# Half rows of the adjacency: read from a bf16 copy in DRAM, or cast from f32 by the load

## The chip, the cores and the metric

One core of a Trainium2 chip runs the whole program; the other cores do nothing. The metric is the device time of one execution in microseconds. The kernel before took 1334.71 us, the median of three runs (1331.9 to 1335.75).

## What is computed

Four graph layers over 2708 nodes with 256 features and one dense 0/1 adjacency, each as x = x + layer(relu(layernorm(x))). Layer 1 is the one that the change touches. The node and edge adjacencies are the same matrix, its diagonal cleared first:

```python
node_adj_norm = node_adj.at[idx, idx].add(-dn)
edge_output = _gru_cell(node_adj_norm @ h, h, edge_Wih, edge_Whh, ...)
# one of three heads
e_plus = leaky_relu(concatenate([hp, hm], axis=1) @ a, ALPHA)[:, 0]
att = jnp.where(edge_adj > 0, e_plus[None, :], NEG_INF)
att = softmax(att, axis=1) * edge_adj @ hW
```

The softmax needs, for each row and head, the maximum of e_plus over the row's neighbours. That is a product of an adjacency row with a row of scores, and a maximum over it.

## The kernel before

The nodes are padded to 2816 = 22 blocks of 128 (NT = 22). A transposed adjacency stays on chip as fp8 (AT), and most of the work reads it. Row maxima need the other orientation, with a node's neighbours along the free dimension; that is what the half rows are for.

The work runs in stages. **Layer 0** is attention with four heads. It has 8 units (two groups of 11 blocks, four heads) of 22 steps. In a step ACT makes thresholds (L811), DVE turns them into masks with the adjacency (L1130, L1136), and PE multiplies 11 blocks by 4 small matmuls of 65 columns (L1619). DVE evicts a unit in the middle of the next (from L1147) and, in the later units, also widens AT (L1171). SP loads a broadcast row of scores for each unit (load_el, L422). POOL meanwhile loads the second half of AT with a cast (L686). Then, paced by the masks built, it casts the 22 row blocks of the f32 adjacency to bf16 and writes them back to DRAM, into AH_D (L689). SP waits for all of these (L465), clears the diagonal of AH_D with one scattered DMA of two-byte elements (L466), and waits for that.

The **edge GRU** has 22 steps. In each, PE multiplies the node sums (L1665), the head products (L1677, L1679) and the gates (L1710, L1717), and DVE and ACT split and evict. POOL computes delta(t) (L703), which needs ACT's tanh (L876) of the same step, and apply(t-1) (L708, L709), in this order. Between these DVE computes the paired maxima, those of heads 0 and 1: 88 maxima over half rows of 1408 elements (row_max, L1316). rows_before(t) spreads them over 20 steps, 4 or 5 in each. In step t DVE runs the step's first maximum, the blend of step t-1 (L1349, L1350), more maxima, support_low and products_low (L1289, L1295, L1298), the step's last maximum, and gru_new (L1340, L1342).

Maximum i of the paired ones uses half row L = i // 2. The half rows lie in two buffers, AROW[:, L % 2], and load L may start once maxima_after(L - 2) = 2(L - 1) maxima are done. SP issues them (load_row, L483 to L488) in its own order among the loads and stores of the step, each behind its wait for that count.

The **attention** has 9 units (three heads, three groups of blocks) of 22 steps m. PE multiplies (L1760, L1761), while ACT and DVE make the weights. The 44 maxima of head 2 are run by DVE at the steps in row_at, one every 9/4 steps, and SP issues the loads there too. What follows is a node GRU, layer 2 and a test of whether layer 3 is needed at all.

Of the kernel before, what the change touches and what calls it, by code (L numbers as in the profile page):

```python
# [8 lines left out]
BF16 = mybir.dt.bfloat16  # L9
# [9 lines left out]
def gnn_stack_kernel(nc, t_in, out):  # L19
# [60 lines left out]
    with ExitStack() as ctx:  # L80
        def sb(name, shape, dt=F32):
            return ctx.enter_context(nc.sbuf_tensor(name, shape, dt))
# [3 lines left out]
        def sem(name):  # L86
            if name not in sems:
                sems[name] = ctx.enter_context(nc.semaphore(name))
            return sems[name]
# [68 lines left out]
        RD = a0.take(11)  # L158
        ZB = a0.take(NT, dt=BF16, size=2)
        NOTB = a0.take(P, dt=FP8, size=1)  # L160
# [7 lines left out]
        HTF = AT[:, :, htf_at:htf_at + 4 * H0 * C0].bitcast(F32)  # L168
        assert NREAL <= (P - 1) * NT
        THRi = THR.bitcast(mybir.dt.int32)  # L170
# [94 lines left out]
        DN = sb("DN", [P, NT])  # L265
        NOTI = sb("NOTI", [P, P])
        identh = sb("identh", [P, P], F16)
# [15 lines left out]
        MN_D = nc.dram_tensor("m_rows", [H1, NT, P], F32, kind="Internal").ap()  # L283
        AH_D = nc.dram_tensor("adj_rows_half", [NT, P, N], BF16, kind="Internal").ap()
        HT_D = nc.dram_tensor("h_turned", [P, NT, 4 * P], F16, kind="Internal").ap()
# [67 lines left out]
        def rows_before(t):  # L353

            return min(PAIRED, -(-PAIRED * t // ROWS_LAST))

        def loads_before(t):

            return max(2, -(-rows_before(t) // 2))

# [7 lines left out]
        def half_of(L):  # L368

            i = L % (2 * NT)  # L370
            return i // 2, i % 2

        def maxima_after(L):

            return 2 * (L + 1) if L < 2 * NT else PAIRED + L + 1 - 2 * NT

        def diagonal_half(t):

            return t // (NT // 2)
# [32 lines left out]
        def _(sp):  # L412
# [49 lines left out]
            def load_halves(to, k, name):  # L462
                sp.dma_start(to, WS_D[k]).then_inc(sem(name), 16)

            sp.wait_ge(sem("rows_h"), 16 * NT)  # L465
            sp.dma_start(AH_D.rearrange("t p n -> (t p n)")[0:(P - 1) * NT * (N + 1)]  # L466
                         .rearrange("(a b c) -> a b c", b=NT, c=N + 1)[:, :, 0:1],
                         ZB[0:P - 1, :].unsqueeze(2), allow_slow_non_contiguous=True).then_inc(sem("rows_z"), 16)
            sp.wait_ge(sem("rows_z"), 16)
            for i in range(4):  # L470
# [11 lines left out]

            def load_row(L):  # L483
                t, c = half_of(L)
                if L >= 2:
                    sp.wait_ge(sem("rmax"), maxima_after(L - 2))
                sp.dma_start(AROW[:, L % 2, :], AH_D[t, :, c * QUARTER:(c + 1) * QUARTER]
                             ).then_inc(sem(f"arow{L % 2}"), 16)  # L488

            def load_scores(to, h):  # L490
# [3 lines left out]
            for t in range(NT):  # L494
                sp.wait_ge(sem("h1"), t + 1)
                sp.dma_start(H_D[:, t, :], H32R[:, t % 8, :]).then_inc(sem(saved_sem(t % 8)), 16)
                if t == 10:
                    load_halves(GWS, 0, "we")
            for L in range(2):
                load_row(L)  # L500
            sp.wait_ge(sem("hts_act"), NT // 2)
# [36 lines left out]
            for t in range(NT):  # L538
                if t + 2 < NT:
                    load_h(t + 2, HR, 0)  # L540
                for L in range(loads_before(t + 1) if t else 2, loads_before(t + 2)):
                    load_row(L)
                if t == NT - 2:
                    save_maxima(0, 2)
                    load_maxima(0)
                sp.wait_ge(sem("hw_lo"), (H1 + 1) * (t + 1))
                sp.dma_start(HW_D[:, :, t, :].rearrange("h p c -> p h c"), HWS[:, t % 2, :, :]
                             ).then_inc(sem(f"hwst{t % 2}"), 16)
                if t == NT - 2:
                    sp.wait_ge(sem("ns_lo"), DC * len(SUP))  # L550
                    sp.wait_ge(sem("nb_mm"), 1)
                    sp.wait_ge(sem("ht_saved"), 16)
                    for i in range(2):
                        sp.wait_ge(sem(f"hwst{i}"), 16 * 9)
                    for c in range(3):
                        load_products(0, c)
            for L in range(2 * NT, 2 * NT + 2):
                load_row(L)
            for i in range(2):
# [11 lines left out]
            for m in range(len(units1) * NT):  # L571
                n, j = divmod(m, NT)
                h, g = units1[n]
                if m in row_at and row_at[m] + 2 < 4 * NT:
                    load_row(row_at[m] + 2)
                if m + 6 in check_at:
# [67 lines left out]
        def _(pool):  # L644
# [9 lines left out]
            pool.memset(ALR, 0.0).then_inc(sem("consts"), 1)  # L654
            link(pool.memset(ZB, 0.0))
            pool.memset(ET[:], 1.0).then_inc(sem("consts"), 1)
# [27 lines left out]
            for t in range(NT):  # L684
                pool.wait_ge(sem("masks_built"), 3 * t + 1)
                pool.dma_start(AT[:, t, GA[0][1] * P:NT * P], adjT[t, :, GA[0][1] * P:NT * P]).then_inc(sem("adj_b"), 16)  # L686
            for t in range(NT):
                pool.wait_ge(sem("masks_built"), 68 + 4 * t)
                pool.dma_start(AH_D[t], t_in["adj"][t * P:(t + 1) * P, :]).then_inc(sem("rows_h"), 16)  # L689

            pool.wait_ge(sem("dn"), 16)
# [3 lines left out]
            for t in range(NT):  # L695
                pool.wait_ge(sem("h1"), t + 1)
                pool.tensor_copy(HHL[:, t, 0, :], H32R[:, t % 8, :]).then_inc(sem("hi1"), 1)

            def delta(t, base, hr, n):

                pool.wait_ge(sem(f"hr{t % 4}"), 16 * (saved_count(t % 4) + (t // 4 + 1) + (len(range(t % 4, NT, 4)) if base else 0)))
                pool.wait_ge(sem("n"), base + t + 1)
                pool.tensor_tensor(hr[:, t % 4, :], hr[:, t % 4, :], n[:, t % 2, :], ALU.subtract).then_inc(sem("delta"), 1)  # L703
# [6 lines left out]

            for t in range(NT + 1):
                if t < NT:
                    delta(t, 0, HR, GT)
                if t >= 1:
                    apply(t - 1, 0, HR)

            pool.wait_ge(sem("hw_mm"), NT)
            for m in range(len(units1) * NT):
                if m in piece_at:
                    i = piece_at[m]  # L720
                    which, _, c, scale = pieces2[i]
                    if i == 0:
                        pool.wait_ge(sem("rmax"), MAXIMA)
                    pool.wait_ge(sem("raw0"), 32 + [16, 32, 48, 64, 96, 128][i])
                    half = [WIH2S, WHH2S, W2S][i // 2][:, c, :, :]
                    split(RAW2, half, scale, 2 * D if which == "W2T" else 3 * D)
# [281 lines left out]
        def _(dve):  # L1008
# [294 lines left out]
            def row_max(i):  # L1303
# [10 lines left out]
                if i > 0:  # L1314
                    dve.wait_ge(sem("rmax"), i)
                dve.tensor_tensor_reduce(junk, AROW[:, L % 2, :], eb[:, c * QUARTER:(c + 1) * QUARTER], 1.0, 0.0,  # L1316
                                         ALU.mult, ALU.max, M2[:, c, h * NT + t:h * NT + t + 1]).then_inc(sem("rmax"), 1)
# [635 lines left out]
```

## Time and profile before

| | |
|---|---|
| median of 3 runs | 1334.71 us |
| the profiled execution | 1334.99 us |
| its span, first to last instruction | 1332.9 us |
| mean granted TensorE clock | 0.941 |
| busy, share of the span | PE 86%, DVE 70%, ACT 59%, POOL 16% |
| moved by the DMA engines | 153.68 MB, mean 115 GB/s |

Busy time is that of one profiled execution. "Issue" as the releaser of a wait means that the engine waited for nothing that the profile shows. PE is the matmuls and PEld the weight loads, which overlap them. In a window an instruction that crosses its edge counts in both. Times are microseconds, or nanoseconds where a mean of one is given.

### The profile page before, as it was taken

To read this page: it belongs to the slowest core of one execution; us is meant where nothing else is said; L and a number is where in the kernel's file an instruction comes from. 1 tells how busy PE (TensorE), PEld (TensorE's weight loads), DVE (VectorE), ACT (ScalarE), POOL (GpSimd) and SP (SyncE) were. 2 spreads that over 40 slices of the span, in tenths; PEclk is the share of its full clock that TensorE was granted. 3 is DMA by queue.
4 is the path that set the end of the run, shared out by engine and by line. 5 is a ranking of instruction groups with operands and counts; after the bars stand their busy time and mean duration, and the time that the engine had idled before them with its cause. 6 is when DMAs were issued, how large, how long until landed. Compare 5 with 4: busy or idle time off the path is not lost.

```text
span 1332.9 us, 35106 instructions
## 1 busy us (share of the span) xinstructions
PE 1140.3 (86%) x15054; PEld 938.5 (70%) x15054; DVE 937.4 (70%) x2037; ACT 785.0 (59%) x1001; POOL 216.7 (16%) x296
## 2 busy tenths in 40 slices
PE   5529897987886989899978999999999997778997
PEld 4429887887885767666656888888888654446886
DVE  5786677767896289999995998769995365553541
ACT  3479988777735123332226999989989465653000
POOL 5631010000003012222222000001220141220000
PEclk9759999999995789999999999999999998899999
DMA  9936565556307343434336345417852010020532
GB/s 216 180 51 67 62 95 115 98 111 128 63 4 267 94 128 100 126 104 129 104 114 210 106 147 180 135 59 286 281 193 104 5 30 16 16 95 1 180 125 86
DMA packets 83731, 153.68 MB, mean 115 GB/s; under 512 B 9537, under 2 KB 60337, under 8 KB 82609
## 3 DMA queue, kind: packets, MB, share of 16 engines
q1 hardware_dynamic: 74993, 127.05, 30.8%
q0 software_dynamic: 7392, 23.79, 12.9%
q8 instruction: 120, 1.97, 0.6%
q10 hardware_dynamic: 1184, 0.53, 0.1%
q14 instruction: 42, 0.34, 0.1%
HBM read 171.26 MB, written 35.60 MB: 155 GB/s over the span
## 4 chain that ended last, share of the span: by engine, by line
PE 56%; DVE 23%; issue 8%; ACT 6%; DMA 3%; POOL 3%; ACTq 0%; SPq 0%; DVEq 0%; POOLq 0%
PE PS L1619 18%; PE PS L1760 10%; PE PS L1761 10%; DVE scratch L1316 9%; PE PS L1814 8%; PE PS L1710 3%; POOL arena L703 2%; PE PS L1801 2%; DVE arena L1298 2%; DVE arena L1090 2%; PE PS L1717 1%; PE PS L1587 1%; DMA arena<-e_rows 1%; DVE arena L1342 1%; PE PS L1654 1%
## 5 line engine op out<-in xcount | busy, mean ns | idle before, releaser
L1760 PE MATMUL PS<-arena 128*128 128x257 f16 x1452 | 325.5, 272 | 7.6 <-ACT arena L897 4.4
L1619 PE MATMUL PS<-arena 128*128 128x65 f16 x7744 | 259.1, 196 | 80.8 <-issue 41.3
L1761 PE MATMUL PS<-arena 128*128 128x257 f16 x1452 | 325.5, 274 | 0.0
L1619 PEld LDWEIGHTS PS<-arena 128*128 128x128 fp8e4 x7744 | 256.4, 99 | 83.4 <-issue 81.6
L811 ACT ACTIVATE arena<-arena 128x1408 fp8e4<-128x1408 f32 x176 | 242.5, 1456 | 51.4 <-DVE arena L1130 51.1
L1316 DVE CUSTOM_DVE_ANT_0 scratch<-arena 128x1408 bf16<-128x1408 bf16 x132 | 223.2, 1691 | 23.7 <-DMA arena<-e_rows 11.1
L897 ACT ACTIVATE arena<-arena 128x896 int16<-128x896 uint8 (+1 forms) x198 | 187.3, 973 | 22.8 <-DVE arena L1371 14.7
L1760 PEld LDWEIGHTS PS<-arena 128*128 128x128 bf16 x1452 | 142.7, 98 | 32.6 <-issue 8.6
L1761 PEld LDWEIGHTS PS<-arena 128*128 128x128 bf16 x1452 | 139.9, 96 | 21.5
L1130 DVE TENSOR_TENSOR arena<-arena,AT 128x352 int32<-128x352 int32 x176 | 91.3, 519 | 83.4 <-PE PS L1619 63.3
L888 ACT ACTIVATE arena<-arena,E1B 128x896 uint8<-128x896 f32 (+1 forms) x131 | 139.3, 1064 | 2.0 <-DMA arena<-m_rows 2.0
L876 ACT ACTIVATE arena<-arena 128x256 f32<-128x256 f32 x44 | 18.3, 417 | 186.1 <-DVE arena L1342 186.1
L1710 PE MATMUL PS<-arena 128*128 128x512 f16 x528 | 122.3, 382 | 0.4 <-ACT PS L860 0.4
L1665 PE MATMUL PS<-AT,arena 128*128 128x256 fp8e4 x968 | 111.5, 275 | 0.0
L703 POOL TENSOR_TENSOR arena<-arena 128x256 f32<-128x256 f32 x44 | 47.4, 1076 | 377.8 <-ACT arena L876 377.8
L1814 PE MATMUL PS<-arena,AT 128*128 128x256 f16 x968 | 106.2, 273 | 0.8 <-DVE X L1466 0.8
L1665 PEld LDWEIGHTS PS<-AT,arena 128*128 128x128 f16 x968 | 95.6, 99 | 12.1
L1814 PEld LDWEIGHTS PS<-arena,AT 128*128 128x128 fp8e4 x968 | 94.6, 98 | 12.5 <-DVE X L1466 1.1
L1371 DVE TENSOR_TENSOR arena<-arena,AT 128x224 int32<-128x224 int32 (+1 forms) x198 | 80.1, 432 | 19.2 <-ACT arena L888 19.0
L1710 PEld LDWEIGHTS PS<-arena 128*128 128x128 f16 x528 | 51.8, 98 | 56.8 <-issue 2.7
L1136 DVE TENSOR_TENSOR arena<-arena,AT 128x352 int32<-128x352 int32 x176 | 90.8, 516 | 0.0
L1423 DVE SCALAR_TENSOR_TENSOR scratch<-arena 128x1408 fp8e4<-128x1408 f32 x44 | 73.2, 1664 | 0.8 <-DMA arena<-in_adj 0.8
(189 smaller groups left out, 1333.3 us busy)
## 6 DMA issues: line engine op xcount, KB each, us to landing
arena<-adj_rows_half SPq DMA_DIRECT2D x88, 352.0 KB, 3.1
arena<-in_adj SPq DMA_DIRECT2D x44, 704.0 KB, 5.3
adj_rows_half<-in_adj POOLq DMA_DIRECT2D x22, 704.0 KB, 8.3
hw_saved<-arena SPq DMA_DIRECT2D x22, 387.0 KB, 4.3
AT<-in_adjT POOLq DMA_DIRECT2D x44, 176.0 KB, 8.0
arena<-hw_saved SPq DMA_DIRECT2D x9, 774.0 KB, 5.8
arena<-el_rows SPq DMA_DIRECT2D x8, 704.0 KB, 11.5
arena<-h_saved SPq DMA_DIRECT2D x44, 128.0 KB, 2.1
```

Source lines behind the costliest of these rows:

```text
L811: act.activation(THR[:, m % NTHR, :], ELB[:, n % 2, :], ACT.Sigmoid, bias=ERB[:, j, h:h + 1], scale=SHARP, saturate=False).then_inc(sem("t ...
L888: act.activation(Y[:, m % NRING, 0:nb * P], MB[n % 2][:, 0:nb * P], ACT.Relu, bias=E1B[:, j * H1 + h:j * H1 + h + 1], saturate=False).then ...
L897: act.activation(PWb[:, m % NRING, 0:nb * P], Y[:, m % NRING, 0:nb * P], ACT.Copy, scale=256.0).then_inc(sem("p_ready"), 1)
L1130: dve.tensor_tensor(mask_words(m, 0), THRi[:, m % NTHR, :], adj_words(m), ALU.bitwise_and).then_inc(sem("m_plus"), 1)
L1136: dve.tensor_tensor(mask_words(m, 1), mask_words(m, 0), adj_words(m), ALU.bitwise_xor).then_inc(sem("masks_built"), 1)
L1316: dve.tensor_tensor_reduce(junk, AROW[:, L % 2, :], eb[:, c * QUARTER:(c + 1) * QUARTER], 1.0, 0.0, ALU.mult, ALU.max, M2[:, c, h * NT + t ...
L1619: ins = pe.matmul(PS[:, first_bank(n) + i, (2 * r + q) * C0:(2 * r + q + 1) * C0], MASK[:, (m + j) % NMASK, q, k * P:(k + 1) * P], MOV[:, ...
L1665: ins = pe.matmul(PS[:, c, 0:D], HHL[:, j, a, c * P:(c + 1) * P], AT[:, j, i0 * P:i1 * P], start=(j == 0 and a == 0), stop=(j == NT - 1 an ...
L1710: ins = pe.matmul(PS[:, bank, :], half(c, a), w[:, c, b, 0:2 * D], start=False, stop=(w is wih and c == DC - 1 and a == 1), skip_group_che ...
L1760: pe.matmul(PS[:, k, 0:D + 1], weights, w[:, 0:D + 1], start=(j == 0), stop=False)
L1761: ins = pe.matmul(PS[:, k, 0:D + 1], weights, w[:, D + 2:2 * D + 3], start=False, stop=(j == NT - 1))
L1814: ins = pe.matmul(o, AT[:, j, t * P:(t + 1) * P], YHL[:, j, a, :], start=(j == 0 and a == 0), stop=(j == NT - 1 and a == 1))
```

## The change

AH_D, its casts, its zeroing and SP's waits for them are gone. POOL issues the loads of the half rows itself, straight from the f32 adjacency; the DMA casts to bf16 on the way into AROW. Their place in POOL's program is set by three conditions around delta and apply, and in the attention by row_at. The diagonal is cleared on chip: before the first maximum that uses a half row which holds the diagonal block (head 0, and again head 2), DVE ANDs that block, 128x64 words, with NOTI, which is now bf16, and waits for the result. That makes 22 ANDs in the edge GRU and 22 in the attention.

```diff
@@ SP
-            sp.wait_ge(sem("rows_h"), 16 * NT)
-            sp.dma_start(AH_D...[:, :, 0:1], ZB[0:P - 1, :].unsqueeze(2), ...).then_inc(sem("rows_z"), 16)
-            sp.wait_ge(sem("rows_z"), 16)
...
-            def load_row(L):
-                t, c = half_of(L)
-                if L >= 2:
-                    sp.wait_ge(sem("rmax"), maxima_after(L - 2))
-                sp.dma_start(AROW[:, L % 2, :], AH_D[t, :, c * QUARTER:(c + 1) * QUARTER]
-                             ).then_inc(sem(f"arow{L % 2}"), 16)
...
-                for L in range(loads_before(t + 1) if t else 2, loads_before(t + 2)):
-                    load_row(L)
...
-                if m in row_at and row_at[m] + 2 < 4 * NT:
-                    load_row(row_at[m] + 2)
@@ POOL
-            link(pool.memset(ZB, 0.0))
...
-            for t in range(NT):
-                pool.wait_ge(sem("masks_built"), 68 + 4 * t)
-                pool.dma_start(AH_D[t], t_in["adj"][t * P:(t + 1) * P, :]).then_inc(sem("rows_h"), 16)
...
+            def load_row(L):
+
+                t, c = half_of(L)
+                if L >= 2:
+                    pool.wait_ge(sem("rmax"), maxima_after(L - 2))
+                pool.dma_start(AROW[:, L % 2, :], t_in["adj"][t * P:(t + 1) * P, c * QUARTER:(c + 1) * QUARTER]
+                               ).then_inc(sem(f"arow{L % 2}"), 16)
+
+            load_row(0)
+            load_row(1)
+            fetched = 2
...
             for t in range(NT + 1):
+                while t < NT and 2 * fetched < rows_before(t + 1):
+                    load_row(fetched)
+                    fetched += 1
                 if t < NT:
                     delta(t, 0, HR, GT)
+                while fetched < 2 * NT + 2 and maxima_after(fetched - 2) <= min(rows_before(t + 1) + 1, rows_before(t + 2)):
+                    load_row(fetched)
+                    fetched += 1
                 if t >= 1:
                     apply(t - 1, 0, HR)
+                while fetched < 2 * NT + 2 and maxima_after(fetched - 2) <= min(rows_before(t + 1) + 2, rows_before(t + 2)):
+                    load_row(fetched)
+                    fetched += 1
...
             for m in range(len(units1) * NT):
+                if m in row_at and row_at[m] + 2 < 4 * NT:
+                    load_row(row_at[m] + 2)
@@ DVE, row_max
+                if h != 1 and c == diagonal_half(t):
+                    at = t * P - c * QUARTER
+                    block = AROW[:, L % 2, at:at + P].bitcast(mybir.dt.int32)
+                    link(dve.tensor_tensor(block, block, NOTI[:].bitcast(mybir.dt.int32), ALU.bitwise_and))
                 dve.tensor_tensor_reduce(junk, AROW[:, L % 2, :], eb[:, c * QUARTER:(c + 1) * QUARTER], 1.0, 0.0,
                                          ALU.mult, ALU.max, ...).then_inc(sem("rmax"), 1)
```

## Rows read from the trace of the kernel before

**Rows 1.** The page, part 4: shares of the chain of waits by line.
```profile
PE PS L1619 18%; PE PS L1760 10%; PE PS L1761 10%; DVE scratch L1316 9%; PE PS L1814 8%; PE PS L1710 3%; POOL arena L703 2%; PE PS L1801 2%; DVE arena L1298 2%; DVE arena L1090 2%; PE PS L1717 1%; PE PS L1587 1%; DMA arena<-e_rows 1%; DVE arena L1342 1%; PE PS L1654 1%
```

**Rows 2.** Busy time by stretch: PE, PEld, DVE, ACT, POOL, clock, DMA share, GB/s.
```profile
190.00:350.00 160.00, 129.12 (x3847) 127.39 (x3844) 113.22 (x258) 123.79 (x91) 12.12 (x23) 0.97 0.62 118
...
470.00:700.00 230.00, 208.18 (x1513) 147.62 (x1512) 211.12 (x354) 66.75 (x152) 56.10 (x55) 0.98 0.39 112
725.00:890.00 165.00, 163.62 (x1463) 141.16 (x1461) 140.42 (x288) 156.46 (x170) 0.00 (x0) 1.00 0.43 132
```

**Rows 3.** Waits, 93 to 372 us: engine, line, releaser: total us, times, longest.
```profile
PE PS L1619 <- issue: 41.3, 23, 3.6
```

**Rows 4.** The chain of waits in layer 0: start us, us, what.
```profile
221.69 3.21 issue
224.90 4.26 PE PS L1619 x128
229.17 3.58 issue
...
337.37 2.26 issue
...
355.23 12.55 PE PS L1619 x389
```

**Rows 5.** DMA queues, 190 to 350 us: packets, MB, share of 16 engines.
```profile
q8 instruction: 30, 0.49, 1.3%
```

**Rows 6.** POOL's casts to DRAM (L689), in the line's own view: ns, then landing.
```profile
L689 POOL DMA_DIRECT2D adj_rows_half<-in_adj x22: 491/493/547, 189.8 to 345.8; - x22
...
DMA to landing us min/median/max: 6.3/8.3/12.5
```

**Rows 7.** The timeline of one step of the edge GRU: start us, us, instruction.
```profile
548.55 1.62 DVE L1316 CUSTOM_DVE_ANT_0 scratch<-arena 128x1408 bf16<-128x1408 bf16 x1
...
549.22 1.53 POOL L703 TENSOR_TENSOR arena<-arena 128x256 f32<-128x256 f32 x1 [7.80 <-ACT arena L876]
...
550.78 0.42 DVE L1349 SCALAR_TENSOR_TENSOR arena<-arena 128x256 f32<-128x256 f32 x1 [0.61 <-POOL arena L703]
...
551.67 2.15 DVE L1316 CUSTOM_DVE_ANT_0 scratch<-arena 128x1408 bf16<-128x1408 bf16 x1
```

**Rows 8.** PE's L1619 alone by stretch: PE, PEld, clock, DMA share, GB/s.
```profile
92.20:190.00 97.80, 87.86 (x2596) 87.19 (x2597) 0.94 0.57 61
190.00:393.50 203.50, 171.18 (x5154) 169.24 (x5150) 0.97 0.51 94
```

**Rows 9.** The page, part 6: count, KB each, median us to landing.
```profile
arena<-el_rows SPq DMA_DIRECT2D x8, 704.0 KB, 11.5
```

**Rows 10.** DVE's timeline at the last unit of layer 0.
```profile
370.49 1.83 DVE L1147 TENSOR_TENSOR arena<-PS,arena 128x390 f32<-128x390 f32 x4
...
375.50 0.52 DVE L1130 TENSOR_TENSOR arena<-arena,AT 128x352 int32<-128x352 int32 x1
...
376.81 0.52 DVE L1130 TENSOR_TENSOR arena<-arena,AT 128x352 int32<-128x352 int32 x1
```

**Rows 11.** The 88 loads of half rows (L487, SP, bf16), the line's own view.
```profile
DMA to landing us min/median/max: 2.8/3.1/9.0
```

**Rows 12.** The loads L686 (POOL, f32 to fp8), then L569 (SP, f32).
```profile
L686 POOL DMA_DIRECT2D AT<-in_adjT x22: 527/530/620, 89.4 to 186.3; - x22
...
DMA to landing us min/median/max: 4.1/4.4/8.7
...
DMA to landing us min/median/max: 3.9/5.3/8.7
```

**Rows 13.** DVE's smallest copy (ns), and a maximum behind another.
```profile
L1295 DVE COPY arena<-FRHL x22: 169/171/684, 476.4 to 708.4; 128x6 f16<-128x6 f16 x22
...
543.09 1.62 DVE L1316 CUSTOM_DVE_ANT_0 scratch<-arena 128x1408 bf16<-128x1408 bf16 x1 [0.17 <-DVE M L1316]
```

**Rows 14.** The 44 maxima of head 2, 725 to 890 us: busy, mean ns, idle before.
```profile
L1316 DVE CUSTOM_DVE_ANT_0 scratch<-arena 128x1408 bf16<-128x1408 bf16 x44 | 71.2, 1619 | 7.7 <-issue 5.3 <-DMA arena<-adj_rows_half 2.4
```

More of the change, by code:

```diff
@@ L158, in gnn_stack_kernel @@
         RD = a0.take(11)
-        ZB = a0.take(NT, dt=BF16, size=2)
         NOTB = a0.take(P, dt=FP8, size=1)
@@ L168, in gnn_stack_kernel @@
         HTF = AT[:, :, htf_at:htf_at + 4 * H0 * C0].bitcast(F32)
-        assert NREAL <= (P - 1) * NT
         THRi = THR.bitcast(mybir.dt.int32)
@@ L265, in gnn_stack_kernel @@
         DN = sb("DN", [P, NT])
-        NOTI = sb("NOTI", [P, P])
+        NOTI = sb("NOTI", [P, P], BF16)
         identh = sb("identh", [P, P], F16)
@@ L283, in gnn_stack_kernel @@
         MN_D = nc.dram_tensor("m_rows", [H1, NT, P], F32, kind="Internal").ap()
-        AH_D = nc.dram_tensor("adj_rows_half", [NT, P, N], BF16, kind="Internal").ap()
         HT_D = nc.dram_tensor("h_turned", [P, NT, 4 * P], F16, kind="Internal").ap()
@@ L355, in rows_before @@
             return min(PAIRED, -(-PAIRED * t // ROWS_LAST))
-        def loads_before(t):
-            return max(2, -(-rows_before(t) // 2))
         check_before = [2, 1, 1]
@@ L463, in load_halves @@
                 sp.dma_start(to, WS_D[k]).then_inc(sem(name), 16)
-            sp.wait_ge(sem("rows_h"), 16 * NT)
-            sp.dma_start(AH_D.rearrange("t p n -> (t p n)")[0:(P - 1) * NT * (N + 1)]
-                         .rearrange("(a b c) -> a b c", b=NT, c=N + 1)[:, :, 0:1],
-                         ZB[0:P - 1, :].unsqueeze(2), allow_slow_non_contiguous=True).then_inc(sem("rows_z"), 16)
-            sp.wait_ge(sem("rows_z"), 16)
             for i in range(4):
@@ L498, in _ @@
                     load_halves(GWS, 0, "we")
-            for L in range(2):
-                load_row(L)
             sp.wait_ge(sem("hts_act"), NT // 2)
@@ L540, in _ @@
                     load_h(t + 2, HR, 0)
-                for L in range(loads_before(t + 1) if t else 2, loads_before(t + 2)):
-                    load_row(L)
                 if t == NT - 2:
@@ L556, in _ @@
                         load_products(0, c)
-            for L in range(2 * NT, 2 * NT + 2):
-                load_row(L)
             for i in range(2):
```

## The prediction

> **What bounds the kernel now.** I read the page's chain of waits by line first: the matmuls of layer 0 (L1619) hold 18% of it, those of the attention (L1760, L1761) 20%, and DVE's row maxima (L1316) 9% [rows 1]. Stages with different limits, then, so the busy time by stage came next. In layer 0 PE is busy for only 129.12 of the 160 us from 190 to 350, although DVE and ACT both have room. From 470 to 700, the edge GRU, DVE is busy 211.12 of 230 us. From 725 to 890, the attention, PE is busy 163.62 of 165 [rows 2]. The change touches all three stages.
>
> Then layer 0 in detail. L1619 stands still for "issue", which is none of the kernel's own waits, 23 times and 41.3 us [rows 3]. In the chain the long ones come every 128 or 256 matmuls, 4.26 us of work at a time; without stops 389 matmuls run in 12.55 us, 32.3 ns each, as they do after 355 [rows 4]. 128 matmuls with their weight loads are 256 instructions, and from 190 to 350 the DMA queue named "instruction" moved 30 packets [rows 5] while PE ran 3847 matmuls and 3844 weight loads [rows 2]: 256 a packet. So I read the stops as PE waiting for its next block of code, and a loaded DMA as what makes it late. The 22 casts (L689) run from 189.8 to 345.8 and take 8.3 us each [rows 6]; PE's longest stops stand in their bursts: 3.21 us at 221.69 and 3.58 at 229.17 [rows 4].
>
> Last, one step of the edge GRU. DVE's order is: first maximum of the step, blend of the step before, further maxima, the subtractions, the last maximum, the new gate. POOL's delta (L703) starts when ACT's tanh ends, takes 1.53 us and ends at 550.75; DVE waits 0.61 us for it, blends in 0.89 us and starts the second maximum at 551.67 [rows 7]. This chain has no slack.
>
> **The change, part by part.** All is told against the profiled execution, 1334.99 us (span 1332.9 and 2.1 around it), 0.3 above the median.
>
> *Layer 0 gets lighter.* From 190 to 393.5 PE issues 5154 matmuls [rows 8]. At 32.3 ns that is 166.5 us, so 37.0 us are lost, stops and the lower clock behind them together; no more than this can come back. Not all will: four of the broadcasts of scores (L422, 704 KB, 11.5 us) also fall in this stretch and stay [rows 9]. Before 190 there are two of them beside the lighter loads of L686, and there 97.8 - 2596 x 0.0323 = 13.9 us were lost [rows 8]; some 4 of it is the cold start, which leaves 5 per broadcast at most. Four broadcasts keep between 0 and 20 us; I take 2.5 each, 10. Another 1 to 2 us go to DVE, which does a step in 1.31 us (375.50 to 376.81) but has each unit's eviction, 5.0 us (370.49 to 375.50), in front of it [rows 10]. The gain: 37 - 10 - 1 = **26 us**, between 15 and 36.
>
> Here a rule speaks against me. The Trainium skill (Runtime: NRT & Kernel Launch, Instruction fetch mechanics) says code comes in 16 KiB blocks over the sequencer's own DMA queue and crossing a block is mostly hidden; by it nothing would come back. The stops every 128 matmuls disagree.
>
> The scattered zeroing (L466) and SP's two waits go too. SP then waits for DVE's last output of layer 0 anyway, the work that covers them; they are worth nothing.
>
> *The row loads move from SP to POOL and cast.* In the paired maxima load L (maxima 2L and 2L+1) needs maximum 2L-3 done. SP issued it then: a 128x1408 bf16 load, 3.1 us to landing, minimum 2.8, [rows 11]; the 2.4 us for which DVE ever waited for one lie in the attention [rows 14]. POOL issues it in its own order, before delta(t), after delta(t) or after apply(t-1). Working through rows_before (0, 5, 9, 14, 18, 22, 27, 31, 36, 40, 44 and the same again), most loads whose buffer came free in the second half of a step are issued only behind the next delta. How long until they land? The nearest row is L686: POOL, cast, 128x1408 f32 from DRAM, 4.1 at least, 4.4 median, 0.53 us of POOL to issue. It writes one byte where the new load writes two. L569, the same f32 bytes uncast from SP, takes 3.9 to 8.7, median 5.3 [rows 12]. I take 4.4, between 4.1 and 5.3. The waits of 44 maxima, ten steps:
> - Needed by the second maximum (6, 10, 28, 32): it starts 0.9 us after the delta ends, so 4.4 - 0.9 = 3.5 us each.
> - Needed by the first (14, 36): it would have started at 548.55; the delta, which could start at 549.22, takes some 0.6 with DVE idle (now it ends 0.6 behind the maximum), and the load lands at 554.2: 5.7 us each, of which the 0.6 us wait for the delta comes back.
> - Needed by the third (20, 24, 42): it starts about 2.9 us after the delta, so 1.5 us each.
>
> Each wait also ends a collision: the second maximum now takes 2.15 us instead of 1.62 beside POOL's apply [rows 7], and 0.5 us comes back. So 4 x 3.0 + 2 x 4.6 + 3 x 1.0 = 24 per ten steps, 48 for twenty, one more third wait at maximum 86: 49 us. PE's cover doesn't help, since the waits stand in DVE's chain.
>
> A sentence by page only: the Trainium skill (DMA: Bandwidth & Descriptors, Anatomy of one DMA) fits a POOL DMA as 2.0 us plus bytes over 436 GB/s, 3.65 us for 704 KB; the sum would be 13 us lower by it, and L686's minimum of 4.1 disagrees.
>
> *The diagonal.* 22 ANDs of 64 words in the GRU, 22 in the attention, each followed by a wait for itself. A 352-word AND takes 0.52 us [rows 10], a 6-element copy 0.171, the wait for a result 0.17 behind a maximum [rows 13]. So one costs 0.17 to 0.69, 4 to 15 us in all; 64 words are near the small end: 22 x 0.3 = 7 us on DVE's chain in the GRU. Together the GRU grows by **56 us**.
>
> *The attention.* A maximum comes every 9/4 steps of a PE-bound loop, and a load has two such distances, over 6 us, less one maximum. DVE waited 2.4 us for the loads at 3.1 [rows 14]. POOL has nothing else to do there. 22 ANDs add 7 us to DVE, which is 85% busy beside a full PE [rows 2]. I take **3 us**, 0 to 6.
>
> Sum: 1335 - 26 + 56 + 3 = **1368 us**. Its own ends: landings of 4.1 and 5.3 change 19 waits by -6 and +17 us, the AND is worth -3 and +8; 1335 - 36 + 47 + 0 = 1346 and 1335 - 15 + 81 + 6 = 1407.
>
> **The rivals.**
> 1. *Nothing comes back in layer 0*, as PE's stops are not due to the casts: 1335 + 59 = 1394. For it: PE also stopped 2.26 us at 337.37, between two bursts. Against: none after 355, once the casts are over [rows 4]. Chance 0.14.
> 2. *The loads land late*, at 6.0 us: the issue is held up by a reduction of 1.62 us, as delta is. 19 waits x 1.6 = 30 more: 1398. Against: POOL's issue takes 0.53 us in layer 0 beside DVE's steady ANDs. The Trainium skill (SBUF — State Buffer, SBUF: two separate sides) knows such a hold-up for VectorE's two-port modes; the trace neither shows nor excludes it for L1316. Chance 0.10.
> 3. *Faster: the load is short.* If it lands as fast as the quickest bf16 load, 2.8 us, the third waits vanish and twelve shrink by 1.6: 56 - 7 - 19 = 30. With layer 0's full 36 and nothing in the attention: 1335 - 36 + 30 = 1329. It decides from a landing of about 3.3 us down, and only with the full return. Against: L686 never below 4.1. Chance 0.12.
>
> **How the numbers follow.** The forecast has 0.64 and names 1368. The range leaves out the corner where all of its worst terms meet, takes in rival 1 and reaches down to rival 3: 1332 to 1398. About 0.3%, 4 us, is what a measurement can tell from no change. Faster: most of rival 3, 0.10. Same: the rest of it and a corner of the forecast, 0.05. Slower: 0.85.
>
> **What would show it.** In layer 0: the issue time of L1619 at 20 us or less and its end near 367. In the GRU: L1316 with idle time released by the DMA from in_adj, near 60 us over some 19 waits; the steps averaging 13 us instead of 10.9 to 12.7; landings of 4.4 us. The AND at 0.2 us, 44 times. The attention unchanged within 6 us. Wrong if L1316 waits under 35 us in all, or if the stops in layer 0 stay at 41.

## The result and the profile after

The kernel after takes **1366.9 us**, the median of four runs (1363.71 to 1371.81), against 1335.23 us for the kernel before beside it on the same chip (1331.9 to 1339.83). The ratio is 1.0241, with an interval of 1.0210 to 1.0271: 2.4% slower. The forecast was 1368 us. Two of its terms were off by more than 10 us each, and their errors cancel.

The profiled executions are 1364.52 us after and 1334.99 before, their spans 1361.2 and 1332.9. So 28.3 us have to be found:

| stage, and how it is bounded | before | after | difference | predicted |
|---|---|---|---|---|
| layer 0: first to last L1619 (after: L1615) | 93.2 to 393.3 | 92.5 to 355.9 | -36.7 | -26 |
| edge GRU: first maximum to last small copy | 243.5 | 297.8 | +54.3 | +56 |
| attention: first to last L1760 (after: L1756) | 331.4 | 346.1 | +14.7 | +3 |
| all else | | | -4.0 | 0 |

The last row is what is left over. The piece behind the attention took 286.9 us before and 283.2 after. In the nine kernels of the experiments it took 285.4 to 287.1, so it is read as the scatter of one execution. The way from layer 0's last matmul to the first maximum is as long as it was (72.1 us against 71.6): the zeroing and SP's waits that went with it were worth nothing, as predicted.

First the page of the kernel after, part 4: the shares of the chain by engine and by line [rows 1].

```profile
PE 48%; DVE 22%; DMA 12%; issue 8%; ACT 6%; POOL 4%; SPq 0%; DVEq 0%; ACTq 0%; POOLq 0%
PE PS L1615 16%; DMA arena<-in_adj 9%; PE PS L1810 8%; PE PS L1756 8%; PE PS L1757 8%; DVE scratch L1312 7%; PE PS L1706 3%; PE PS L1797 2%; POOL arena L684 2%; DVE arena L1290 2%; DVE arena L1082 2%; PE PS L1713 1%; DMA arena<-e_rows 1%; DVE arena L1338 1%; PE PS L1650 1%
```

The loads from in_adj were on no row of this list before. They hold 9% of the chain now, second only to layer 0's matmuls. Layer 0 itself went from 18% to 16%.

**Layer 0.** PE's waits from 90 to 372 us [rows 3]: total, times, longest.

```profile
DVE arena L1122 <- PE PS L1615: 32.3, 15, 4.3
...
PE PS L1615 <- issue: 11.8, 7, 3.5
```

The stops by "issue" fell from 41.3 us in 23 to 11.8 us in 7. DVE waits less for PE too: its masks (L1122, L1130 in the kernel before) had waited for it 31 times, 63.3 us. The chain of waits shows where the seven are [rows 4].

```profile
119.91 2.80 issue
...
150.91 3.54 issue
154.45 38.18 PE PS L1615 x1151
192.63 1.77 issue
194.40 89.89 PE PS L1615 x2815
284.29 0.61 issue
284.90 31.44 PE PS L1615 x984
```

The long ones stand before 194, in the stretch of the loads of AT. Behind it 2815 matmuls run in one piece, at 89.89/2815 = 31.9 ns each. Three broadcasts of scores fall between 194 and 355 and land in 5.4 us; PE stops beside them for 0.61 us at most. A fourth goes out at 183.5, beside the last loads of AT, and the stop of 1.77 us comes as it lands. The window over this stretch [rows 8] and the broadcasts in it:

```profile
194.00:355.00 161.00, 159.74 (x5001) 159.50 (x5001) 143.43 (x333) 142.65 (x108) 0.00 (x0) 1.00 0.07 18
```
```profile
arena<-el_rows SPq DMA_DIRECT2D x3, 704.0 KB, 5.4
```

The mean granted clock is 1.00 and the DMA share 0.07; over the same stretch of the kernel before they were 0.97 and 0.58.

**The edge GRU.** Waits from 420 to 720 us:

```profile
DVE scratch L1312 <- DMA arena<-in_adj: 27.7, 9, 6.0
DVE arena L1311 <- DMA arena<-in_adj: 27.5, 10, 5.7
...
DVE arena L1345 <- POOL arena L684: 10.5, 16, 1.4
```

A maximum that needs a freshly cleared half row waits at the AND (L1311), the others at the reduction (L1312). Together that is 55.2 us in 19 waits. One of them, first DVE and then POOL in the timeline [rows 7]:

```profile
443.24 1.62 DVE L1312 CUSTOM_DVE_ANT_0 scratch<-arena 128x1408 bf16<-128x1408 bf16 x1
...
445.48 0.43 DVE L1345 SCALAR_TENSOR_TENSOR arena<-arena 128x256 f32<-128x256 f32 x1 [0.61 <-POOL arena L684]
...
449.55 1.63 DVE L1312 CUSTOM_DVE_ANT_0 scratch<-arena 128x1408 bf16<-128x1408 bf16 x1 [3.19 <-DMA arena<-in_adj]
```
```profile
443.92 1.52 POOL L684 TENSOR_TENSOR arena<-arena 128x256 f32<-128x256 f32 x1 [7.56 <-ACT arena L868]
...
445.40 1.11 POOL L673 DMA_DIRECT2D arena<-in_adj  x2
```

POOL sat 7.56 us waiting for ACT's tanh. The buffer had been free for part of that time, but the load's issue stands behind delta in POOL's program. It is issued at 445.40 and DVE stands from 446.36 to 449.55. The lines' own views give the load [rows 11, 12] and the AND:

```profile
L673 POOL DMA_DIRECT2D arena<-in_adj x88: 527/537/825, 388.8 to 912.9; - x88
...
DMA to landing us min/median/max: 4.1/4.4/9.1
```
```profile
L1311 DVE TENSOR_TENSOR arena<-arena,NOTI x44: 211/224/227, 427.7 to 917.4; 128x64 int32<-128x64 int32 x44
```

**The attention.** Waits from 755 to 930 us:

```profile
ACT arena L889 <- DVE arena L1367: 20.6, 13, 4.0
DVE arena L1311 <- DMA arena<-in_adj: 16.2, 12, 5.4
PEld PS L1756 <- ACT arena L889: 11.6, 3, 5.0
PE PS L1756 <- DVE arena L1408: 10.8, 3, 4.7
DVE scratch L1312 <- DMA arena<-in_adj: 9.7, 7, 4.5
```

Where DVE had waited 2.4 us for a half row [rows 14], it now waits 16.2 + 9.7 = 25.9 us. The other rows show how this reaches PE. DVE stands in front of its masks (L1367), ACT waits for these, and PE waits for ACT's weights and for DVE's evictions. The windows of the two stages say the same [rows 2]: from 755 to 925 PE is busy 158.83 of 170 us, where it had been 163.62 of 165.

```profile
433.00:725.00 292.00, 239.17 (x1559) 159.39 (x1557) 217.29 (x385) 70.88 (x161) 75.78 (x104) 0.89 0.44 92
755.00:925.00 170.00, 158.83 (x1375) 135.60 (x1373) 137.65 (x296) 146.43 (x159) 23.21 (x40) 0.96 0.65 119
```

### The profile page after: what moved, and what is told of

Its sections match the earlier page's. It is cut to its first block, busy times and chain, and to the rows that moved or that the text cites. A ratio compares the mean times of both kernels' runs of the same rounds, so it can differ in the third digit from the quotient of the medians.

```text
span 1361.2 us, 35126 instructions
## 1 busy us (share of the span) xinstructions
PE 1156.2 (85%) x15054; PEld 940.5 (69%) x15054; DVE 943.7 (69%) x2081; ACT 784.4 (58%) x1001; POOL 248.0 (18%) x361
## 4 chain that ended last, share of the span: by engine, by line
PE 48%; DVE 22%; DMA 12%; issue 8%; ACT 6%; POOL 4%; SPq 0%; DVEq 0%; ACTq 0%; POOLq 0%
PE PS L1615 16%; DMA arena<-in_adj 9%; PE PS L1810 8%; PE PS L1756 8%; PE PS L1757 8%; DVE scratch L1312 7%; PE PS L1706 3%; PE PS L1797 2%; POOL arena L684 2%; DVE arena L1290 2%; DVE arena L1082 2%; PE PS L1713 1%; DMA arena<-e_rows 1%; DVE arena L1338 1%; PE PS L1650 1%
## 5 line engine op out<-in xcount | busy, mean ns | idle before, releaser
L1756 PE MATMUL PS<-arena 128*128 128x257 f16 x1452 | 330.6, 275 | 17.3 <-DVE arena L1408 10.8
L1757 PE MATMUL PS<-arena 128*128 128x257 f16 x1452 | 330.4, 277 | 0.0
L1615 PE MATMUL PS<-arena 128*128 128x65 f16 x7744 | 251.7, 194 | 52.7 <-DVE arena L1128 40.9
L1615 PEld LDWEIGHTS PS<-arena 128*128 128x128 fp8e4 x7744 | 250.6, 98 | 53.7 <-issue 53.3
L803 ACT ACTIVATE arena<-arena 128x1408 fp8e4<-128x1408 f32 x176 | 240.5, 1455 | 17.8 <-DVE arena L1122 17.8
L1312 DVE CUSTOM_DVE_ANT_0 scratch<-arena 128x1408 bf16<-128x1408 bf16 x132 | 217.7, 1649 | 46.2 <-DMA arena<-in_adj 37.3
L889 ACT ACTIVATE arena<-arena 128x896 int16<-128x896 uint8 (+1 forms) x198 | 187.4, 972 | 36.7 <-DVE arena L1367 28.4
L1756 PEld LDWEIGHTS PS<-arena 128*128 128x128 bf16 x1452 | 144.0, 99 | 42.9 <-ACT arena L889 13.4
L868 ACT ACTIVATE arena<-arena 128x256 f32<-128x256 f32 x44 | 18.3, 416 | 221.5 <-DVE arena L1338 221.5
L1706 PE MATMUL PS<-arena 128*128 128x512 f16 x528 | 127.8, 394 | 0.6 <-ACT PS L852 0.6
L1122 DVE TENSOR_TENSOR arena<-arena,AT 128x352 int32<-128x352 int32 x176 | 91.2, 518 | 49.4 <-PE PS L1615 32.3
L1673 PE MATMUL PS<-arena 128*128 128x512 f16 x132 | 63.3, 502 | 52.8 <-DVE arena L1290 52.8
L684 POOL TENSOR_TENSOR arena<-arena 128x256 f32<-128x256 f32 x44 | 44.6, 1014 | 325.9 <-ACT arena L868 325.9
L673 POOL DMA_DIRECT2D arena<-in_adj x88 | 51.0, 579 | 234.8 <-DVE M L1312 234.8
```

Of the source, the lines that this page charges most:

```text
L803: act.activation(THR[:, m % NTHR, :], ELB[:, n % 2, :], ACT.Sigmoid, bias=ERB[:, j, h:h + 1], scale=SHARP, saturate=False).then_inc(sem("t ...
L889: act.activation(PWb[:, m % NRING, 0:nb * P], Y[:, m % NRING, 0:nb * P], ACT.Copy, scale=256.0).then_inc(sem("p_ready"), 1)
L1122: dve.tensor_tensor(mask_words(m, 0), THRi[:, m % NTHR, :], adj_words(m), ALU.bitwise_and).then_inc(sem("m_plus"), 1)
L1615: ins = pe.matmul(PS[:, first_bank(n) + i, (2 * r + q) * C0:(2 * r + q + 1) * C0], MASK[:, (m + j) % NMASK, q, k * P:(k + 1) * P], MOV[:, ...
L1706: ins = pe.matmul(PS[:, bank, :], half(c, a), w[:, c, b, 0:2 * D], start=False, stop=(w is wih and c == DC - 1 and a == 1), skip_group_che ...
L1756: pe.matmul(PS[:, k, 0:D + 1], weights, w[:, 0:D + 1], start=(j == 0), stop=False)
```

## The experiments

The stages below are bounded as in the table above. "The kernel before" is always the one that ran beside.

### Do the casts make PE stop in layer 0?

**a_casts_back.** The kernel after, with the 22 casts to DRAM put back and read by nobody.

```diff
+            for t in range(NT):
+                pool.wait_ge(sem("masks_built"), 68 + 4 * t)
+                pool.dma_start(AH_D[t], t_in["adj"][t * P:(t + 1) * P, :]).then_inc(sem("rows_h"), 16)
             pool.wait_ge(sem("dn"), 16)
```

Expected:

> The changed kernel with the 22 casts of adjacency rows put back into POOL's program where they were (masks built 68 + 4t), written to a DRAM tensor that nothing reads. Theory (the casts' traffic makes PE wait for its code in layer 0): PE's layer 0 matmuls end near 393 instead of 356, 'issue' before them is near 41 us instead of 12, and the run is 35 to 38 us longer than the changed kernel, near 1404. Rival (the 37 us came from something else in the edit, such as the scattered zeroing or SP's waits): the end of layer 0 stays near 356 and the run near 1367.

Measured: 1403.09 us (1400.86 to 1405.49), 1.0513 times the kernel before (1.0477 to 1.0549). Layer 0 takes 301.5 us again, as before the change (300.1), and its matmuls stop by "issue" for 40.1 us. The group in the page:

```profile
L1619 PE MATMUL PS<-arena 128*128 128x65 f16 x7744 | 261.6, 197 | 79.7 <-issue 40.1
```

So the casts alone cost 38 us of layer 0, all that the change had won there, and rival 1 falls. The size is good to some 4 us: in the five kernels with all 22 casts the stage takes 296.0 (b_and) to 304.3 us (b_pool_rows), in the four without them 261.5 to 264.2. The run also prices the new loads by themselves: with layer 0 as it was, they and the ANDs cost 5.1%.

**b_paced.** The kernel before, with the same casts let go by the masks that PE has used up rather than by those built.

```diff
-                pool.wait_ge(sem("masks_built"), 68 + 4 * t)
+                pool.wait_ge(sem("mask_used"), 52 + 4 * t)
```

> The kernel before with its 22 casts paced by PE's progress (mask_used 52 + 4t) instead of by the masks built, so that they come evenly, one every 5.7 us, and end at the same place. If bursts of casts are what stops PE: 'issue' in layer 0 falls from 41 to 20 to 30 us and the run to 1315 to 1325. If the bytes moved count, however spread: 'issue' stays at 38 to 45 and the run within 5 us of before.

Measured: 1335.44 us (1327.9 to 1347.59), ratio 0.9982 (0.9954 to 1.0011). PE's waits from 90 to 400 us:

```profile
PE PS L1619 <- issue: 39.2, 21, 5.7
```

The stops stayed (41.3 before), and so did the time. But the edit did not do what was meant by it, one cast every 5.7 us. The casts still go out 0.8 to 13.8 us apart (3.5 to 15.8 before), and they still meet the broadcasts. So this run does not tell what evenly spaced casts would cost; it shows only that the other count changes nothing.

**a_casts_half.** The kernel after, with every second cast put back (11 of 22).

```diff
+            for t in range(0, NT, 2):
+                pool.wait_ge(sem("masks_built"), 68 + 4 * t)
+                pool.dma_start(AH_D[t], t_in["adj"][t * P:(t + 1) * P, :]).then_inc(sem("rows_h"), 16)
```

> The changed kernel with every second of the 22 casts put back (masks built 68 + 8t'), read by nothing. If a cast costs by its bytes: half of the 38 us of a_casts_back returns, layer 0's matmuls end near 375. If only overlapping casts stop PE, less than a quarter returns and they end at 356 to 365.

Measured, in a single execution: 1398.74 us, layer 0 at 288.5 us, that is +25.1 for half the casts where the whole cost +38.1. The second expectation (less than a quarter) is out. The first (half, 19) is missed by 6 us, in a stage that scatters by some 4 from kernel to kernel. The three longest stops in the chain behind 194:

```profile
228.13 4.47 issue
...
264.39 3.57 issue
...
302.79 3.79 issue
```

Each stands where a broadcast of scores and a cast run together. The broadcasts go out at 220.75, 258.63 and 296.33 and land 8.8, 7.5 and 10.7 us later; the casts nearest to the stops go out at 222.07, 262.99 and 302.44. The kernel before shows the same: of its stops behind 190 the four of 3 us and more (at 221.69, 229.17, 266.32 and 302.41) all fall in the flight of a broadcast (issued at 218.7, 258.9 and 298.7, landing 18.3, 17.8 and 15.9 us later).

**a_casts_clear.** The kernel after with 11 casts again, at moments between the broadcasts.

```diff
+            for t, m in enumerate((74, 79, 96, 101, 118, 123, 140, 145, 150, 155, 160)):
+                pool.wait_ge(sem("masks_built"), m)
+                pool.dma_start(AH_D[t], t_in["adj"][t * P:(t + 1) * P, :]).then_inc(sem("rows_h"), 16)
```

> As a_casts_half, 11 casts put back into the changed kernel, but at masks built 74, 79, 96, 101, 118, 123 and then 140 to 160 by 5, so that hardly one runs beside a broadcast of scores (which start near 66, 88, 110 and 132). a_casts_half gave back 26 of the 38 us, with stops of 3.6 to 4.9 us where a broadcast and a cast met. Theory (a cast beside a broadcast is what makes code late; alone it costs about 1 us, as the six behind 325 us in the kernel before): layer 0's matmuls end near 366, and no stop is over 2.5 us behind 194. Rival (each cast costs alike, wherever it stands): they end near 382.

Measured, in a single execution: 1386.64 us, layer 0 at 280.3 us, +16.9, or 1.5 us for each cast against 2.3 in a_casts_half. The longest stop behind 194 in the chain is 2.53 us, it starts before the broadcast of 252.9 goes out, and no stop in the chain starts in the flight of any of the three broadcasts (issued at 220.7, 252.9 and 289.2, landing some 7 us later). So a cast costs something away from the broadcasts, and the stops over 3 us stand where both run. Whether the stage as a whole loses more by it is not shown: 280.3 and 288.5 are one execution each, and they differ by no more than the five kernels with all the casts do (8.3 us). PE's waits by "issue" in the two kernels, a_casts_half first:

```profile
PE PS L1619 <- issue: 28.1, 15, 4.9
```
```profile
PE PS L1619 <- issue: 24.6, 18, 3.3
```

### Where do the 54 us of the GRU come from?

**b_pool_rows.** The kernel before, casts and scattered zeroing included, with the loads moved from SP to the very places of the kernel after in POOL's program. They still read AH_D, so no load casts and nothing is ANDed.

```diff
@@ SP
...
-                for L in range(loads_before(t + 1) if t else 2, loads_before(t + 2)):
-                    load_row(L)
...
@@ POOL, with the three conditions of the kernel after
...
+                pool.dma_start(AROW[:, L % 2, :], AH_D[t, :, c * QUARTER:(c + 1) * QUARTER]
+                               ).then_inc(sem(f"arow{L % 2}"), 16)
```

> The kernel before, with only the issue of the half-row loads moved to POOL, at the changed kernel's places; they still read the bf16 copy, uncast, and there is no AND. Theory (place costs): layer 0 as before; the waits in the GRU are there, smaller by the shorter landing. With 3.6 us to landing (3.1 and POOL's 0.5) they come to about 35 us, the run to 1365 to 1375. Rival (cast or landing costs): the GRU within 10 us of before, the run near 1342. The attention tells what part of its 15 us is the place: by the theory of crowded landings it stays within 4 us of before, as half the bytes are read.

Measured: 1367.11 us (1359.8 to 1369.05), ratio 1.0227 (1.0185 to 1.0269). The GRU grew by 31.0 us to 274.5, the attention by 1.1. DVE's waits in the GRU, 420 to 720 us, and the loads' own view:

```profile
DVE scratch L1325 <- DMA arena<-adj_rows_half: 36.0, 12, 4.6
```
```profile
DMA to landing us min/median/max: 3.1/3.3/7.4
```

The place alone costs 31 us, although these loads land as fast as SP's did (median 3.3 against 3.1). Twelve maxima wait, where 19 did in the kernel after.

**b_and.** The kernel before, with the 44 ANDs and nothing else.

```diff
+                if h != 1 and c == diagonal_half(t):
+                    at = t * P - c * QUARTER
+                    block = AROW[:, L % 2, at:at + P].bitcast(mybir.dt.int32)
+                    link(dve.tensor_tensor(block, block, NOTI[:].bitcast(mybir.dt.int32), ALU.bitwise_and))
```

> The kernel before with the 44 ANDs of the diagonal block added on DVE (the diagonal is clear already, so nothing changes in the values). Theory: 22 x 0.3 = 6 to 7 us more in the GRU, under 2 in the attention, the run near 1342. Rival (the ANDs are what made the attention 15 us longer): the attention alone grows by 8 or more and the run is over 1350.

Measured: 1343.18 us over ten runs (1336.89 to 1349.75), ratio 1.0067 (1.0042 to 1.0092), about 8 us. The GRU grew by 4.7 us, which is 0.21 us for each of its 22 ANDs; the attention by 0.4, within a full PE's cover. The span is 5.3 us longer than before's in the profiled executions; the interval reaches down to 0.42%, 5.6 us, so the profile stands just under its lower end.

Of +54.3 that leaves 54.3 - 31.0 - 4.7 = 18.6 us for the longer landing of the cast load. The waits say the same: 55.2 - 36.0 = 19.2. Twelve of them are 1.1 us longer each (4.4 - 3.3), 13 in all; the other seven, 0.7 to 1.4 us each and 6.3 together, are not there at all when a load lands in 3.3.

**a_order.** The kernel after with one condition replaced, so that POOL issues a load ahead of delta(t) whenever its buffer comes free before the step's last maxima.

```diff
-                while t < NT and 2 * fetched < rows_before(t + 1):
+                while t < NT and fetched < 2 * NT + 2 and maxima_after(fetched - 2) <= rows_before(t + 1):
```

> The changed kernel with one condition changed: ahead of delta(t) POOL issues every load whose buffer is free by rows_before(t + 1) maxima, instead of only those that step t needs. Theory (the place in POOL's program costs, not the cast): the maxima's waits for in_adj in the GRU fall from 55 us to under 10, the GRU is 42 to 48 us shorter than in the changed kernel and 7 to 12 longer than before, the attention keeps its 15 us, and the run is near 1322. Rival (the longer landing costs): the waits stay above 35 us and the run above 1350.

Measured: **1317.82 us** (1315.06 to 1320.6), ratio 0.9869 (0.9836 to 0.9902): 1.3% faster than the kernel before. POOL's timeline over the same step as above:

```profile
439.52 0.53 POOL L673 DMA_DIRECT2D arena<-in_adj  x1 [3.09 <-DVE M L1312]
...
444.00 1.52 POOL L684 TENSOR_TENSOR arena<-arena 128x256 f32<-128x256 f32 x1 [3.95 <-ACT arena L868]
445.47 0.57 POOL L673 DMA_DIRECT2D arena<-in_adj  x1
```

The load leaves at 439.52, during what had been POOL's wait for the tanh, and delta still starts at 444.00. The GRU takes 250.4 us, +6.9 over the kernel before, with 4.7 of it the ANDs, and not one maximum waits for in_adj there. The landing did not change. The same cast load that "cost" 18.6 us costs at most the 2.2 us that are left once it leaves early, so the place is the cause and the length only multiplies it. The attention stayed as it was in the kernel after: 345.6 us, with all the waits for in_adj that were left. From 686 to 900:

```profile
DVE arena L1311 <- DMA arena<-in_adj: 17.4, 11, 4.8
DVE scratch L1312 <- DMA arena<-in_adj: 8.6, 8, 3.9
```

### The attention, and a better version

**a_attn3.** a_order, and a third half-row buffer for head 2 only, in room of the arena that is free by then. A load of head 2 now needs the maximum three back, not two.

```diff
+        AROW3 = tmp.take(QUARTER, dt=BF16, size=2)
...
-                    pool.wait_ge(sem("rmax"), maxima_after(L - 2))
+                    pool.wait_ge(sem("rmax"), maxima_after(L - (2 if L < 2 * NT + 2 else 3)))
...
+            load_row(2 * NT + 2)
             for m in range(len(units1) * NT):
-                if m in row_at and row_at[m] + 2 < 4 * NT:
-                    load_row(row_at[m] + 2)
+                if m in row_at and row_at[m] + 3 < 4 * NT:
+                    load_row(row_at[m] + 3)
...
```

> The reordered kernel (a_order) with a third half-row buffer for head 2 alone, in the space of EB that is free by then; a load there may start once the maximum three before it is done. Theory (in the attention the casting loads land up to 8 us after their issue beside other transfers, and two buffers give them 5; the maxima then hold DVE's masks and so PE): the 26 us of waits for in_adj fall under 6, the attention goes from 346 us back to 331 to 335, and the run is near 1305. Rival (the casting traffic itself, or DVE's load, makes the attention longer): it stays near 346 and the run near 1318.

Measured: **1307.95 us** (1305.93 to 1312.85), ratio 0.9774 (0.9743 to 0.9805): 2.3% faster than the kernel before, which took 1339.48 us beside it, and the best version here. The attention takes 333.2 us, +1.8 over before. The maxima's line (L1326), and the window of the attention:

```profile
  DMA arena<-in_adj: 2.6, 1
```
```profile
710.00:860.00 150.00, 148.51 (x1326) 127.77 (x1325) 135.45 (x290) 141.87 (x155) 23.01 (x40) 1.00 0.74 135
```

PE is full again, at a clock of 1.00. All but 1.8 of the 14.7 us of the attention were due to the loads coming late: the ANDs and the bytes of the cast loads are all still there.

**a_at_clear.** a_attn3, with the loads of AT's second half let go at other counts, meant to lie between the broadcasts and to win some of the 11 us of stops, most of them before 194.

```diff
+            at_load = [1 + 2 * t for t in range(8)] + [30 + 2 * t for t in range(6)] + [52 + 2 * t for t in range(6)] + [74, 76]
...
-                pool.wait_ge(sem("masks_built"), 3 * t + 1)
+                pool.wait_ge(sem("masks_built"), at_load[t])
```

> The reordered kernel with the third buffer (a_attn3), and the 22 loads of AT's second half moved out of the way of the two broadcasts that they now meet: at masks built 1 to 15, 30 to 40 and 52 to 62 by 2, then 74 and 76, instead of every third. Theory (the same collision costs some 8 us ahead of 190): 'issue' in layer 0 falls from 11 to 3 to 6 us and the run to 1300 to 1304. Rival (these loads, at a share of 0.57 of the DMA engines, don't matter for the stops): no change from a_attn3's 1308.

Measured: 1310.86 us (1306.73 to 1315.56), ratio 0.9793 (0.9761 to 0.9825), with layer 0 at 261.5 us against 264.2, and stops of 9.6 us against 10.8. The time is that of a_attn3. But only the first of the three broadcasts came clear. The second goes out at 148.9 and the third at 185.1, each with three loads of AT around it; the middle ones, from POOL's timeline:

```profile
148.53 0.53 POOL L673 DMA_DIRECT2D AT<-in_adjT  x1 [1.21 <-DVE arena L1143]
...
184.68 0.53 POOL L673 DMA_DIRECT2D AT<-in_adjT  x1 [1.21 <-DVE arena L1143]
```

The two longest stops in the chain, 2.48 us at 157.98 and 1.94 us at 190.43, stand in the flight of these two. So the edit did not separate loads and broadcasts, and whether doing so would win anything is open.

## Why the prediction was right, and where it was not

**Layer 0, -26 predicted, -37 measured.** The mechanism held: the stops were due to the casts, and with the casts back they were back (a_casts_back). The term that failed is the one for what stays: "Four broadcasts keep between 0 and 20 us; I take 2.5 each, 10." They kept about 1: from 190 to 356.2 the 5114 matmuls take 166.2 us, where 32.3 ns each make 165.2. What the text gave as the most that can come back, 37.0 us, came back almost whole. I had sized a broadcast by the loss before 190, where it runs beside the loads of AT, and carried that to a stretch where three of the four would run alone. The stops show the difference: beside a cast up to 4.47 us in one place, alone at most 0.61. The 1 us that I gave to DVE does not show either; behind 194 L1615 waits 0.2 us for DVE.

The rule that I set against it is the Trainium skill's (Runtime: NRT & Kernel Launch, Instruction fetch mechanics), that crossing a block of code is mostly hidden. If the stops are the fetch of code, it does not hold in this stage: adding 22 casts took 38 us, with stops of up to 5.9 us (a_casts_back). That they are is still an inference, from their spacing of 128 or 256 matmuls, from one packet for 256 of PE's instructions, and from their coming and going with the casts; the trace has no record that ties a stop to a packet.

**The edge GRU, +56 predicted, +54.3 measured.** Every step of it is in the profile. Which loads would be issued behind delta was worked out from rows_before, as 19 waits in all: there are 19, 18 of them at the maxima named and at those 44 further on. The nineteenth was put at maximum 86, which the list already had (42 + 44); it stands at maximum 46, so in the number 19 there was some luck:

```profile
579.35 0.23 DVE L1311 TENSOR_TENSOR arena<-arena,NOTI 128x64 int32<-128x64 int32 x1 [0.85 <-DMA arena<-in_adj]
```

The waits hold 55.2 us. The prediction had 3.5, 5.7 and 1.5 us each for the three kinds, 61 us in all; they measure 3.2, 5.8 and 0.9 in the mean (8, 4 and 7 waits). With 4.7 us for the ANDs that makes 59.9 us, of which the GRU grew by 54.3; so 5.6 us came back elsewhere, where the prediction had counted on 12 from collisions and from delta. The landing, taken from L686 at 4.4 us, is 4.4 us with the same minimum of 4.1, though it writes twice the bytes. The fit by page only (Trainium skill, DMA: Bandwidth & Descriptors, Anatomy of one DMA), 3.65 us for 704 KB, stays under even the fastest of the 88. (What the sum would lose by it is 19 x 0.75 = 14 us, not the 13 of the prediction.) The AND, taken as 0.3 with its wait, takes 0.22 by itself and cost 0.21 in b_and.

**The attention, +3 predicted, +14.7 measured.** The step that failed is "a load has two such distances, over 6 us, less one maximum". It is right on average, and a wait does not go by the average. Two bits of the kernel after show it, DVE and then POOL:

```profile
877.72 1.62 DVE L1312 CUSTOM_DVE_ANT_0 scratch<-arena 128x1408 bf16<-128x1408 bf16 x1
...
880.68 1.63 DVE L1312 CUSTOM_DVE_ANT_0 scratch<-arena 128x1408 bf16<-128x1408 bf16 x1
...
884.09 0.23 DVE L1311 TENSOR_TENSOR arena<-arena,NOTI 128x64 int32<-128x64 int32 x1 [1.10 <-DMA arena<-in_adj]
```
```profile
879.65 0.82 POOL L673 DMA_DIRECT2D arena<-in_adj  x1 [2.61 <-DVE M L1312]
```

Here the maxima follow each other 3.0 us apart. The load that goes at 879.65, once the maximum of 877.72 is done, is wanted at 884.09 - 1.10 = 882.99, that is 3.3 us later. It lands some 4.4 us after its issue, which is the median, and that is late. A load of 3.1 us, as SP's were, fits such a gap. The longer waits are landings above the median. The load of 764.56 holds DVE until 773.16, for 4.51 us:

```profile
764.56 0.76 POOL L673 DMA_DIRECT2D arena<-in_adj  x1 [2.35 <-DVE M L1312]
```
```profile
773.16 1.63 DVE L1312 CUSTOM_DVE_ANT_0 scratch<-arena 128x1408 bf16<-128x1408 bf16 x1 [4.51 <-DMA arena<-in_adj]
```

SP had started four loads between 763.8 and 765.4, of m_rows and of the node GRU's biases. The DMA issues from 757 to 775:

```profile
arena<-in_adj POOLq DMA_DIRECT2D x4, 352.0 KB, 6.0
arena<-m_rows SPq DMA_DIRECT2D x1, 448.0 KB, 5.5
```

I had a figure for this spread, 3.9 to 8.7 us for L569 [rows 12], and used it for the GRU's bounds alone. I also put DVE's waits under PE's cover ("85% busy beside a full PE"); a wait of 4 us in front of the masks is more than that cover.

That it is the load's length and not POOL that matters here is shown by b_pool_rows: the same places in POOL's program with a landing of 3.3 us cost the attention 1.1 us, and a_order, with the longer landing, cost 14.2. The ANDs cost 0.4 (b_and). So the sign that the prediction named for this stage, unchanged within 6 us, did not come true.

**The sum.** -37 + 54 + 15 - 4 = 28, against -26 + 56 + 3 = 33. The forecast was 1368 and the median is 1366.9, closer than its steps deserve, and that is luck: one term was 11 us too small in gain, one 12 too small in loss.

**The rivals.** Rival 1 (nothing comes back) is refuted by a_casts_back. Rival 2 (landing at 6.0 us, as the issue is held up by a reduction) and rival 3 (landing at 2.8) both fall with a median of 4.4 us. POOL's issue takes 0.54 us in the median beside DVE's maxima, as it did in layer 0, so the hold-up that the Trainium skill describes for two-port modes (SBUF — State Buffer, SBUF: two separate sides) did not reach it. A faster kernel was there to be had, though in a form that I did not name: not by a shorter load but by the same load issued earlier.

## What to carry to other kernels

- When a transfer moves to another engine's in-order program, ask first what stands ahead of its issue there. Here POOL waited 7.6 us for a tanh, for part of it with a free buffer to fill; one condition moved 49 us, and the time went from 2.4% above the kernel before to 1.3% below.
- A ring of two buffers is sized by the shortest gap between uses and by the long tail of the landings, not by their means. A third buffer where the gap was tight took 12 us off the attention (345.6 to 333.2).
- Bytes that nothing waits for can still cost: 22 background casts cost PE 38 us through stops that the kernel's own waits do not explain.

## What the runs showed of the hardware that was not expected

- Broadcasts of 704 KB beside a PE that runs 32 ns matmuls cost nothing alone (at most 0.61 us in 161), yet where one met a cast PE stopped for 3.6 to 4.5 us. Eleven casts cost 25 of the 38 us, and 17 when moved away from the broadcasts, one execution each, in a stage that scatters by some 4 us. The law behind this is open: the number of casts counts, the longest stops stand in the overlap, and what overlap costs in all is not shown.
- A load that casts f32 to bf16 (128x1408) lands in 4.4 us at the median, as did the one that casts f32 to fp8 with half the bytes written. The bf16 load without a cast, from the same queue, takes 3.3. So the bytes read, or the cast, set the time, and the bytes written do not; the runs do not part the two.
- In the GRU PE's mean granted clock fell from 0.98 to 0.89 as its busy share fell from 91% [rows 2] to 82%, and was 0.96 again in a_order, with PE 90% busy. PE holds only some 5 us of that stage's chain of 298, so the clock explains next to none of the 54.

A third buffer for the paired maxima in the GRU was not tried, nor were casts that are truly evenly spaced.
